# Head of a fused attention kernel: x in four loads, the root table loaded first, half of the query weight copied on GpSimd

## The reference

```python
x = x + cross_attention(layernorm(x), ctx, ctx)      # 16 heads of 32, softmax over head and batch together (axis 0)
x = x + relative_attention(layernorm(x))             # 16 heads, tables Eq, Ek, Ev indexed by clipped distance
x = x + gated_attention(layernorm(x))                # normalised queries, softmax, top-3 gates, projection
def _layernorm(x, eps=1e-5): return (x - mean(x)) / sqrt(var(x) + eps)
q = (query @ Wq + bq); k = (key @ Wk + bk); v = (value @ Wv + bv)   # in cross_attention, query = layernorm(x)
```

## Time and profile before

| | before |
|---|---|
| median of 3 runs | 744.22 us |
| lowest, highest | 742.63, 744.83 us |
| profiled execution | 745.07 us, of which 743.1 us are the span |
| mean granted TensorE clock | 0.993 |
| TensorE matmul busy | 716.2 us (96%) |
| VectorE, ScalarE, GpSimd busy | 628.5, 490.5, 502.0 us |

### The profile page before, as it was taken

How to read it: one execution, slowest core, us unless ns; L and a number is a source line. 1 busy time by engine, 2 the same in 40 slices (tenths; PEclk the granted TensorE clock), 3 DMA queues, 4 the chain that set the end, 5 groups by cost and what they waited for, 6 DMA issues and landing times.

```text
span 743.1 us, 17302 instructions
## 1 busy us (share of the span) xinstructions
PE 716.2 (96%) x7542; PEld 569.6 (77%) x7542; DVE 628.5 (85%) x514; ACT 490.5 (66%) x694; POOL 502.0 (68%) x282
## 2 busy tenths in 40 slices
PE   8999999999999999999999999999988999889988
PEld 7777777777787777877777787777766667767876
DVE  5479999999999999999999999999965468887685
ACT  5578577786776877777786776867724445635681
POOL 0165969899898988989889898997992020063300
PEclk9999999999999999999999999999999999999999
DMA  8310110101011010110101101010011799521101
GB/s 334 115 59 1 58 57 2 57 2 57 15 45 58 2 58 1 58 58 1 59 1 59 36 24 58 2 57 2 2 58 57 275 395 367 233 101 58 58 2 57
DMA packets 15339, 55.71 MB, mean 75 GB/s; under 512 B 1696, under 2 KB 2080, under 8 KB 11680
## 3 DMA queue, kind: packets, MB, share of 16 engines
q1 hardware_dynamic: 15264, 54.61, 20.2%
HBM read 43.13 MB, written 11.47 MB: 73 GB/s over the span
## 4 chain that ended last, share of the span: by engine, by line
PE 80%; DVE 12%; ACT 5%; issue 3%; POOL 0%; ACTq 0%; DVEq 0%; POOLq 0%
PE ps L389 25%; PE ps L370 24%; PE ps L478 9%; PE ps L505 7%; PE ps L378 2%; PE ps L626 2%; PE ps L427 2%; DVE blocks L1498 1%; PE ps L739 1%; ACT v_buf L921 1%; DVE extra L1392 1%; DVE extra L1421 1%; DVE ps L1421 1%; PE ps L529 1%; DVE s_buf L1414 1%
## 5 line engine op out<-in xcount | busy, mean ns | idle before, releaser
L1261 POOL TENSOR_TENSOR s_buf<-s_buf,r_all 128x1024 f32<-128x1024 f32 x93 | 197.2, 2162 | 3.6 <-DVE r_all L1434 3.6
L945 ACT ACTIVATE s_buf<-s_buf 128x1024 f32<-128x1024 f32 x128 | 135.7, 1065 | 9.9 <-DVE s_buf L1414 9.1
L929 ACT COPY s_buf<-ps 128x1024 f32<-128x1024 f32 x128 | 123.3, 1018 | 20.6 <-PE ps L478 20.6
L1392 DVE TENSOR_REDUCE extra<-s_buf 128x128 f32<-128x2048 f32 x48 | 109.5, 2281 | 10.5 <-ACT s_buf L929 10.5
L1414 DVE TENSOR_TENSOR s_buf<-s_buf,ps 128x2048 f32<-128x2048 f32 x48 | 106.9, 2283 | 0.5
L1239 POOL TENSOR_TENSOR w_lo<-raw,w_hi 128x2048 fp32r<-128x2048 f32 x6 | 27.5, 4590 | 95.6 <-ACT w_hi L896 95.6
L921 ACT COPY v_buf<-ps 128x512 f32<-128x512 f32 x64 | 37.6, 588 | 78.9 <-PE ps L389 59.4
L1228 POOL TENSOR_TENSOR v_buf<-v_buf,extra 128x512 f32<-128x512 f32 x64 | 81.2, 1313 | 9.4 <-ACT v_buf L921 9.4
L1421 DVE TENSOR_REDUCE ps<-s_buf 128x128 f32<-128x4096 f32 x16 | 70.8, 4428 | 17.5 <-ACT s_buf L945 17.5
L1234 POOL TENSOR_TENSOR odd_lo<-extra,odd_hi 128x512 fp32r<-128x512 f32 x32 | 41.1, 1310 | 54.8 <-ACT odd_hi L904 54.8
L478 PE MATMUL ps<-q_t,k_t 32*128 32x128 f32 x2048 | 75.1, 283 | 2.3 <-ACT v_buf L921 0.6
(11 more groups left out here) (221 smaller groups left out, 1449.9 us busy)
## 6 DMA issues: line engine op xcount, KB each, us to landing
rel_scratch<-blocks SPq DMA_DIRECT2D x16, 636.0 KB, 10.9
s_buf<-rel_scratch SPq DMA_DIRECT2D x7, 1210.0 KB, 10.0
raw<-in_ctxT SPq DMA_DIRECT2D x8, 1024.0 KB, 4.9
extra<-in_ctxT SPq DMA_DIRECT2D x8, 1024.0 KB, 4.9
raw<-in_Wq SPq DMA_DIRECT2D x2, 1024.0 KB, 6.5
raw<-in_Wv SPq DMA_DIRECT2D x2, 1024.0 KB, 4.8
extra<-in_EvRel SPq DMA_DIRECT2D x1, 2048.0 KB, 12.6
extra<-rel_scratch SPq DMA_DIRECT2D x1, 1210.0 KB, 10.2
```

Of the source, the lines that this page charges most:

```text
L929: copy(piece(t, 2 * w + u).rearrange("p e (u n) -> p (e u) n", u=2), ps[:, 2 * u:2 * u + 2, :]).then_inc(s["s_evac"], 1)
L945: nc.scalar.activation(piece(t, p), piece(t, p), ACT.Exp).then_inc(s["exp_done"], 1)
L1261: pool.tensor_tensor(part, part, spread(r_all, 4), ALU.mult).then_inc(s["attn_pool"], 1)
L1392: nc.vector.tensor_reduce(m_ps if k == 0 else m_next[:, k % 2, :], over_pairs(t, 2 * k, 2), AX.XY, ALU.max).then_inc(s["max_done"], 1)
```

## The change

Four edits. SP issues `x` as four transfers of 256 KB, one for each member and each with a semaphore of its own, and VectorE waits before each `moments(0, b)` only for its member; the order of the eight steps of the norm stays. VectorE writes `eps` without waiting for a transfer. ScalarE runs a root of `eps` into an unused cell at once, so that the table load stands first in its list, and then the four roots one behind the other. The query weight's chunks 2 and 3 are rounded by GpSimd, behind a wait for `wq_in`; ScalarE rounds chunks 0 and 1, after its copy of the first transposed member.

```diff
-            x_rows = a["x"].rearrange("b q e -> q b e")
-            load(x_res[:], x_rows, "x_in")
+            for b in range(B):
+                load(x_res[:, b, :], a["x"][b], f"x_in_{b}")
...
-            def query_weight(n):
-                act.wait_ge(s["wq_in"], 16)
-                part = slice(2 * n, 2 * n + 2)
-                copy(wq_hi[:, part], wq_raw[:, part]).then_inc(s["wq_split"], 1)
-
-            ln_std(0, 0)
-            ln_std(0, 1)
-            query_weight(0)
-            ln_std(0, 2)
-            query_weight(1)
-            ln_std(0, 3)
-            for b in range(B):
+            nc.scalar.activation(gtmp[:, 1, 7:8], eps, ACT.Sqrt).then_inc(s["eps_done"], 1)
+            act.wait_ge(s["eps_done"], 2)
+            for b in range(B):
+                ln_std(0, b)
+            for b in range(B):
+                if b == 1:
+                    act.wait_ge(s["wq_in"], 16)
+                    copy(wq_hi[:, 0:2], wq_raw[:, 0:2]).then_inc(s["wq_split"], 1)
                 act.wait_ge(s["tr_done"], b + 1)
                 copy(xq_hi[:, :, b * P:(b + 1) * P],
...
+            pool.wait_ge(s["wq_in"], 16)
+            pool.tensor_copy(wq_hi[:, 2:4], wq_raw[:, 2:4]).then_inc(s["wq_split"], 1)
             pool.wait_ge(s["bv_in"], 16)
...
-            dve.wait_ge(s["x_in"], 16)
             nc.vector.memset(eps, EPS).then_inc(s["eps_done"], 1)
-            for b in range(B):
+
+            def moments0(b):
+                dve.wait_ge(s[f"x_in_{b}"], 16)
                 moments(0, b)
-                if b >= 1:
-                    normalised(0, b - 1)
-            normalised(0, B - 1)
+
+            moments0(0)
+            moments0(1)
+            normalised(0, 0)
+            moments0(2)
+            normalised(0, 1)
+            moments0(3)
+            normalised(0, 2)
+            normalised(0, 3)
```

More of the change, by code:

```diff
@@ L230, in probs_t @@
             return blocks[:, u * B:(u + 1) * B]
-        names = """x_in wq_in wk_in wv_in cols_in bv_in bo_in tab_in ctx_in_0 ctx_in_1 ctx_hi ctx_lo wq_split xq_split wkv_hi wkv_lo wraw_in wodd_in wsplit_hi wsplit_lo wo_lo
+        names = """x_in_0 x_in_1 x_in_2 x_in_3 wq_in wk_in wv_in cols_in bv_in bo_in tab_in ctx_in_0 ctx_in_1 ctx_hi ctx_lo wq_split xq_split wkv_hi wkv_lo wraw_in wodd_in wsplit_hi wsplit_lo wo_lo
             tab_mul ones_done pos_psum pos_done x_hi_done x_lo_done small_in
```

## The result

| | before | changed |
|---|---|---|
| median (22 runs each) | 743.74 us | 742.36 us |
| lowest, highest | 741.38, 745.10 | 740.44, 743.05 |
| profiled execution, its span | 745.07, 743.1 us | 742.31, 740.1 us |
| ratio, 95% interval | | 0.9980 [0.9973, 0.9987] |

The kernel became faster by 1.38 us between the medians, 0.9 to 2.0 us by the interval. Forecast were 1.35 us and 742.9 us. The gain is under the 0.3% that the prediction took as the least that can be told, but the interval leaves out "no change".

What follows compares the result with a forecast made beforehand. TensorE's warming matmuls, then four transpose groups, were to bound the start, passing 1.35 us of VectorE's 2.8 us gain: 744.22 - 1.35 = 742.9 us, range 741.1 to 744.7, likeliest verdict "no difference".

Steps and rivals of the forecast that it cites:

- The bound of the changed kernel: Start of the kernel: TensorE's warming matmuls, unmoved by the change, let the fourth transpose group start at 12.14 instead of 13.49.
- the head: Stretch before the query projection, which started at 14.77 us; forecast to shorten by 1.35 us, moving everything behind by that much.
- the step: Forecast step on what is late next: VectorE wins 2.8 us, but TensorE's warming lets only 1.35 us through.
- The sum: Whole kernel: median 744.22 minus 1.35 gives 742.9 us; from the profiled execution, 745.07 minus 1.35 gives 743.7 us.
- x's landing: Load of x at the start: four quarters forecast to land at 4.4, 5.0, 5.6 and 6.2 us, 0.6 us apart.
- The later loads: Loads issued behind x: query weight forecast to land still at 8.64 us, those behind it where they were.
- GpSimd's rounding: Rounding of half the query weight on GpSimd: forecast 2.16 us, from 8.7 to 10.9, needed at 13.4.
- Rival D: Start of the projection: a GpSimd copy over 6.1 us makes the kernel slower; at 9 us, 747.1 us; chance 0.04.
- Rival B: In the norm, GpSimd's rounding and VectorE hinder each other; VectorE stands 2.16 us, gain 0.8, 743.4 us; chance 0.1.
- Rival A: At the start, warming matmuls end earlier than in the trace; gains of 2.2 us and more, about 741.5 us; chance 0.2.
- Rival C: In the loop, TensorE's lower-clock stretches shift or lengthen, 1 to 2 us; gain eaten, 744.2 us; chance 0.11.
- Rival E: x's four transfers land together near 6.2 us; gain still 1.2 us, 743.0 us; chance 0.55 shared with the forecast.

Runs made afterwards that it cites:

- e0: The changed kernel, unaltered, run again on the chip of later runs: median 742.43 us, against 743.89 for the kernel before beside it.
- e5: The changed kernel with 14 instead of 22 warming matmuls at the start: median 741.02 us, against 743.89 for the kernel before beside it.
- e6: e5 with ScalarE's rounding of the weight ahead of the fourth copy instead of the second: median 741.31 us, against 743.89 for the kernel before.
- e10: e6 with GpSimd's rounding held until VectorE has written the last normalised member: median 741.10 us, against 744.00 for the kernel before.
- e2: The kernel before with x in four transfers, eps written early, root table and weight rounding as before: median 742.42 us, against 743.46 before.
- e9: The kernel before with x in four transfers and the root table first, weight rounding still on ScalarE between the roots: 743.14 us, against 744.00 before.
- e3: The kernel before with only the weight edit: second half rounded on GpSimd, first on ScalarE behind the first transposed member: 744.46 us, against 743.46 before.
- e11: e3 with GpSimd's rounding held until VectorE's last normalised member: median 744.07 us, against 744.00 for the kernel before.
- e4: The changed kernel with x as one transfer again, eps still early: median 743.31 us, against 743.46 for the kernel before.
- e1: The kernel before with only the root table loaded first and eps written without waiting for x: median 742.88 us, against 743.46 before.

## Why the prediction was right

**The bound of the changed kernel.** Forecast: the warming matmuls, not the norm, with 1.35 us of VectorE's gain coming through. Shown: no group waits in the changed kernel, and eight warming matmuls more take 1.43 us in the head. Eight fewer put the projection 0.3 to 0.9 us before that of e0 (e5, e6, e10), up to the next bound. VectorE won 3.7 us (2.8 forecast), and what it won beyond TensorE's share is lost, as the step said.

**The sum.** 13.42 was forecast for the projection, 13.11 and 12.73 were seen. The first group came at 9.19 (9.32 forecast) and the distance of groups is 0.88 us where I took 0.94 from a pair in which the third had waited. ScalarE had 0.24 us in hand at the fourth copy and not 0.08, because I read the 1.73 us of three copies as back to back. Between the medians it is 1.38 us against 1.35 forecast, and this closeness is in part luck. In the two profiled executions the head gained 1.66 and 2.04 us, and at equal granted clock the kernel gains 1.7 to 2.5 us (e0 beside before); more runs at the low clock hide some of it. A term too small (the head) and one left out of the sum (the clock) offset each other.

**x's landing.** Forecast 4.4, measured 3.5. I spread the time of one large transfer evenly over its quarters, and 3.5 lies about midway between the lower end, 2.8, and that. The third quarter was not earlier than forecast: in e10 VectorE waits for it until 6.01 (5.6 forecast). None of this changed the head, since the norm had 2.4 us of slack.

**The later loads.** Wrong. The query weight was to stay at 8.64; it landed at 9.8 (9.1 to 9.9 over all kernels with four transfers, 8.6 to 8.9 with one). The value weight came at 17.7 to 20.0 instead of 17.7 to 18.0. It cost nothing in the changed kernel, because ScalarE was at its first copy out of PSUM until 10.3; it is the bound of e2, e5 and e9. In e5 the projection starts 2.56 us behind the landing. By that distance (an estimate) the weight's chain would end at 12.35 in the changed kernel, 0.76 us before 13.11.

**GpSimd's rounding.** Forecast 2.16, measured 1.04 us, and nothing waited for it. Rival D (6.1 us or more) falls. The Trainium skill, "GPSIMD Engine Reference", section "Engine selection", says that one-input operations run at about line rate there; the 1.04 us for 1024 columns agree, beside VectorE's 2.29 us for 2048.

**Rival B** has a mechanism that is real, which I had called open: 0.46 us in e3, 0.85 us in e6, both gone when GpSimd starts later (e10, e11). By the 0.28 us (e6) VectorE stood still until the rounding was over, as the rival was priced. The Trainium skill, "GPSIMD Engine Reference", section "Specifications", puts this contention to VectorE's instructions "in a 2-port perf mode or with two SBUF inputs". The trace agrees that the two engines contend; no row shows the mode in which the tensor_scalar, with one large input, ran. It didn't strike the changed kernel's profiled execution, since the late weight put GpSimd at 9.79, behind VectorE's 9.47. That was luck. By the forecast they would have met (rounding from 8.7, norm until 10.4); the landing came 1.1 us later than forecast and the norm ended 0.9 us earlier. Had they met, it would have cost little, because the norm had 2.4 us of slack.

**Rival A** is real as well: the 44 records of the warming matmuls took 7.95, 7.89, 7.83, 7.47, 7.45, 7.02, 6.83, 6.69 and 6.67 us in nine executions. The 7.95 are the kernel before, the execution from which the forecast took its term, and the longest of all. The projection came 0.31 and 0.69 us before the forecast 13.42 in the two profiled executions of the changed kernel; 0.13 and 0.51 us of that are the warming, and 0.18 us the distance of the groups. How much more it gains when they end at 8.2 us, no profile of the changed kernel shows; by the weight's chain (a landing at 9.1 to 9.9 plus 2.56 us, an estimate) the projection could start at 11.7 to 12.5 at the earliest. **Rival C** didn't take the gain, but it may have taken a part: in the profiled pair the clock added 1.3 us, and over the runs of e0 the gain at equal clock is larger than that between the medians. **Rival E** falls: VectorE started at 3.51, and at 6.42 with x in one transfer (e4). Its price was also too high a gain, since it took the fourth group from the last member: the fourth follows the third by 0.94 us (e1, e4).

**What the prediction missed** is how the three edits hang together. Measured alone they give 0.6, 1.0 and -1.0 us between the medians; together 1.4. These medians alone don't prove it, for the interval of each is over 1 us wide; the timelines do. x in four needs the weight moved from between the roots (e9), and the moved weight needs x early (e4). A sum of parts would have been wrong; taking the latest of the chains was right, though I left one chain (roots before copies) out because x in four hides it.

**A faster version.** e5 is the simplest: 14 warming matmuls instead of 22, 0.34% [0.22%, 0.47%] under before. The three kernels with 14 (17 runs) have medians of 741.0 to 741.3 us, the two series of the changed kernel (32 runs) 742.4. In e5 the weight's landing is the next bound: to move it, its load would have to go ahead of a part of x, which was not tried.

## What to carry to other kernels

Where a stage's end is the latest of several chains, write down the end of each chain in the changed kernel, each engine's own list order and the distance between its steps among them, and not the share of each edit. Warming matmuls are a fixed stretch ahead of the first real work: when the work behind them comes earlier, shorten them, or the gain ends there. A difference of two profiled executions is split along the chain of waits first, since falls of TensorE's clock of over 1 us come and go between executions. A median that meets the forecast doesn't confirm its terms: compare at equal clock as well.

## What the runs showed of the hardware

- The same 44 records of matmuls, starting at 1.52 us, took between 6.67 and 7.95 us. In each of before, the changed kernel, e0, e1 and e3 seven of them take 1.67 to 1.70 us at 3.2 us and six take 0.83 us at 7.4 us, while the granted clock reads 1.00 in all windows from 2 to 8 us; here the distance of the matmuls tells the level, and the column doesn't.
- A tensor_scalar of 128x512 on VectorE took 0.55 us alone and 0.58, 1.01 and 1.40 us beside a rounding copy of 128x1024 on GpSimd. Each time it ended 0.28 us after the copy, and the copy kept its 1.04 us. A bn_stats of 128x512 beside the copy kept its 0.69 us (e4).
- TensorE idle for 1.97 us in the head, once the 44 records had ended at 8.19, was followed by granted clock 0.50 at 12 to 14 us (e3); 0.70 us of idle was not (e11), nor were 1.53 us ahead of the projection (e5). Around 84 us TensorE stands still for about 1.8 us in both kernels of the profiled pair, and the clock fell behind it in one and not in the other.
- One load of 1024 KB, sent as four of 256 KB, gave its first quarter 2.7 us earlier (first bn_stats at 3.51 instead of 6.24). The load behind it landed at 9.1 to 9.9 us in eight executions instead of 8.6 to 8.9 us in five.
